# A two-layer attention and feed-forward kernel: its preparation divided anew among the engines, the context turned by VectorE

## The reference

```
x = x + L0_xattn(layernorm(x), ctx_512)     # 16 heads; this case's change is in its preparation and its last step
x = x + L0_ffn(layernorm(x))                # the top 64 of 256 rows of each sequence through a 256-1024-256 net
x = x + L1_xattn(layernorm(x), ctx_512)     # 16 heads of 16, causal
x = x + L1_ffn(layernorm(x))                # 8 experts and a shared one

def L0_xattn(hidden_q, kv_c):
    q_big = rope(einsum(hidden_q @ Wq.T, w_kc_q))        # 16 heads of 192
    kv_r  = kv_c * cos + rotate_half(kv_c) * sin         # the context, turned
    scores = (q_big @ W_qr) @ (kv_r @ W_kr).T
    ctx_lat = (softmax(scores) @ kv_r) @ w_kc_kv.T
    return ctx_lat @ Wo.T
```

## Time and profile before

| | |
|---|---|
| median of three runs | 1833.09 us (1830.51 to 1841.44) |
| profiled execution | 1842.96 us, span 1841.1 us |
| busy: TensorE (PE), VectorE (DVE) | 1665.8 us (90%), 1365.5 us (74%) |
| busy: ScalarE (ACT), GpSimd (POOL) | 993.2 us (54%), 941.7 us (51%) |
| mean granted TensorE clock | 0.944 of full speed |

### The profile page before, as it was taken

How to read it: one execution, slowest core, us unless ns; L and a number is a source line. 1 busy time by engine, 2 the same in 40 slices (tenths; PEclk the granted TensorE clock), 3 DMA queues, 4 the chain that set the end, 5 groups by cost and what they waited for, 6 DMA issues and landing times. The chain is left out here.

```text
span 1841.1 us, 48720 instructions
## 1 busy us (share of the span) xinstructions
PE 1665.8 (90%) x16216; PEld 1327.9 (72%) x16216; DVE 1365.5 (74%) x2952; ACT 993.2 (54%) x1983; POOL 941.7 (51%) x625
## 2 busy tenths in 40 slices
PE   6437999999999999999999999996958889997898
PEld 5334888888888888888888888886846445556676
DVE  6876888888888888888888888885664468884223
ACT  5233666666666666666666666662212356662111
POOL 2802777777777777777777777771000221211321
PEclk8557999999999999999999999998979889997999
DMA  9422122112112112122122124128410000004234
GB/s 269 149 63 65 51 61 79 51 56 82 49 59 84 49 57 79 53 60 78 50 65 71 53 67 139 51 73 258 138 53 2 22 26 12 11 12 167 90 122 155
DMA packets 150138, 144.14 MB, mean 78 GB/s; under 512 B 41290, under 2 KB 137208, under 8 KB 149584
## 3 DMA queue, kind: packets, MB, share of 16 engines
q1 hardware_dynamic: 144144, 135.33, 24.6%
q10 hardware_dynamic: 4416, 4.29, 0.7%
q0 software_dynamic: 1536, 3.99, 0.6%
HBM read 92.01 MB, written 33.98 MB: 68 GB/s over the span
## 5 line engine op out<-in xcount | busy, mean ns | idle before, releaser
L1059 POOL TENSOR_TENSOR c_rest<-c_prob 128x1024 f16<-128x1024 f32 (+1 forms) x513 | 796.1, 1572 | 315.4 <-ACT c_prob L902 302.7
L978 DVE TENSOR_REDUCE c_mxp<-c_psM 128x1 f32<-128x400 f32 (+1 forms) x1040 | 588.9, 573 | 114.4 <-PE c_psM L762 99.7
L902 ACT ACTIVATE c_prob<-c_psS,ln,c_exp_scale 128x1024 f32<-128x1024 f32 (+1 forms) x514 | 536.3, 1044 | 243.8 <-PE c_psS L778 238.8
L778 PE MATMUL c_psS<-c_q,c_kk 128*128 128x256 f16 (+1 forms) x3350 | 512.7, 272 | 1.7 <-ACT c_prob L902 1.6
L796 PE MATMUL c_psV<-c_vb,c_prob 128*128 128x129 f16 (+1 forms) x3328 | 396.5, 222 | 0.5 <-POOL c_rest L1059 0.5
L778 PEld LDWEIGHTS c_psS<-c_q,c_kk 128*128 128x128 f16 (+1 forms) x3350 | 321.7, 99 | 87.5 <-ACT c_prob L902 2.2
L799 PE MATMUL c_psV<-c_vb,c_rest 128*128 128x65 f16 (+1 forms) x3328 | 374.2, 193 | 0.0
L762 PE MATMUL c_psM<-c_kkm,c_q 128*128 128x400 f16 (+1 forms) x1040 | 347.5, 335 | 6.1 <-DVE c_mxp L978 3.9
L799 PEld LDWEIGHTS c_psV<-c_vb,c_rest 128*128 128x128 f16 (+1 forms) x3328 | 301.4, 99 | 22.1
L796 PEld LDWEIGHTS c_psV<-c_vb,c_prob 128*128 128x128 bf16 (+1 forms) x3328 | 305.3, 97 | 14.6 <-POOL c_rest L1059 0.7
L724 PE MATMUL c_psQ<-c_xb,c_w2s 128*128 128x256 f16 x1188 | 164.3, 275 | 4.2 <-DVE c_roped L946 2.5
(11 more groups left out here) (294 smaller groups left out, 2187.3 us busy)
## 6 DMA issues: line engine op xcount, KB each, us to landing
c_w2s<-w_scr SPq DMA_DIRECT2D x67, 256.0 KB, 2.6
acc_scr<-c_acc SPq DMA_DIRECT2D x128, 129.0 KB, 2.2
c_ms<-m_scr SPq DMA_DIRECT2D x67, 192.0 KB, 2.3
c_w2s<-w_scr SPq DMA_DIRECT2D x67, 128.0 KB, 2.0
kv<-acc_scr SPq DMA_DIRECT2D x4, 2064.0 KB, 10.3
d_acc<-acc_scr SPq DMA_DIRECT2D x4, 2064.0 KB, 8.3
m_w<-in_L_ffn_W SPq DMA_DIRECT2D x16, 352.0 KB, 4.2
c_vb<-V SPq DMA_DIRECT2D x27, 129.0 KB, 2.0
```

The source lines that it names most:

```text
L778: mm = pe.matmul(psS[g % 2][0:r, i * S:(i + 1) * S], src[:, (lo + i) * P:(lo + i) * P + r], mov[slot][:, :], start=(one == 0 and i % 2 == ...
L902: nc.scalar.activation(prob[g][0:r, 0:w], psS[g % 2][0:r, 0:w], ACT.Exp, bias=keep["ln1024"][0:r, :], scale=exp_scale[slot][0:r, :]).then_ ...
L978: nc.vector.tensor_reduce(mxp[:, st, c:c + 1], psM[:, st, 0:CHUNKS[c][1]], AX.X, ALU.max).then_inc(mx_done, 1)
L1059: nc.gpsimd.tensor_tensor(rest[g][0:r, 0:w], prob[g][0:r, 0:w], high[0:r, 0:w], ALU.subtract).then_inc(rest_done, 1)
```

## The change

In the preparation:
- the context's loads are moved up: batch 0 and the tables behind the first two groups of weights, batch 1 behind the third, the others ahead of Wo and w_kc_kv;
- VectorE takes the largest absolute values from the context as it arrives, before it is turned (`top_of`); GpSimd's maximum over partitions follows in the first block, and the key scale is made there too, with a factor of 1.4143 for what turning can add;
- ScalarE writes the high parts of the weights, and the copies and squares of m straight from PSUM; VectorE keeps the rests;
- GpSimd turns nothing any more; VectorE turns all 8 batches, behind the rests;
- the normalised x is made behind that, and the value products (`wvo`) are last on TensorE and VectorE, their store last on SP.

In the projection x is loaded by SP behind the second batch's sums, the wait for it stands in `add_rows`, and TensorE raises its starting semaphores before it waits for its loads.

The diff, cut to its core:

```diff
         def _(sp):
-            for g in range(H0 // 4):
+            def load_weights(g):
                 heads = slice(4 * g, 4 * g + 4)
                 sp.dma_start(wq[:, heads], t["L0_xattn_Wq"].rearrange("(h k) d -> k h d", h=H0)[:, heads]
                              ).then_inc(in_q[g], 16)
                 sp.dma_start(wkcq[:, heads], t["L0_xattn_w_kc_q"].rearrange("h k q -> k h q")[:, heads]
                              ).then_inc(in_q[g], 16)
...
-            sp.wait_ge(kv_zeroed, 1)
             def load_context(b):
...
+            load_weights(0)
+            load_weights(1)
+            sp.wait_ge(kv_zeroed, 1)
             load_context(0)
+            sp.dma_start(cosk[:], t["cosk"]).then_inc(in_t, 16)
+            sp.dma_start(sink[:], t["sink"]).then_inc(in_t, 16)
+            load_weights(2)
+            load_context(1)
+            load_weights(3)
+            sp.dma_start(ident[:], t["ident"]).then_inc(in_r, 16)
+            sp.dma_start(wqr[:], t["L0_xattn_W_qr"].rearrange("h (e q) r -> q h e r", e=2)).then_inc(in_r, 16)
+            sp.dma_start(wkr[:], t["L0_xattn_W_kr"].rearrange("h d r -> d h r")).then_inc(in_r, 16)
+            for b in range(2, B):
+                load_context(b)
             sp.dma_start(wo[:], t["L0_xattn_Wo"].rearrange("(c e) k -> e c k", e=P)).then_inc(in_o, 16)
             sp.dma_start(wkckv[:], t["L0_xattn_w_kc_kv"].rearrange("h k d -> k h d")).then_inc(in_o, 16)
-            for b in range(1, B):
-                load_context(b)
...
-            sp.wait_ge(w2p_done, 3 * H0)
+            sp.wait_ge(w_high, 3 * NP0)
+            sp.wait_ge(w_low, 3 * NP0)
             sp.dma_start(t["w2_scr"].rearrange("g p c -> p g c"),
                          wqk[:, 0:H0 * DK * DCQ].rearrange("p (g c) -> p g c", g=NP0)).then_inc(stored, 16)
-            sp.wait_ge(d_done, D_NM)
-            sp.dma_start(t["wvo_scr"], wvo[:]).then_inc(stored, 16)
...
+            sp.wait_ge(d_done, D_VO + N_VO)
+            sp.dma_start(t["wvo_scr"], wvo[:]).then_inc(stored, 16)
...
         @block.gpsimd
...
-            pool.wait_ge(in_t, 32)
-            h = DC // 2
-            for b in range(B):
-                r = rot[b % 2]
-                pool.wait_ge(in_k[b], 32)
-                if b >= 2:
-                    pool.wait_ge(roped, b - 1)
-                nc.gpsimd.tensor_tensor(r[:, :, 0:h], kv[:, b, :, h:DC], sink[:, :, 0:h],
-                                        ALU.mult).then_inc(rotated, 1)
-                nc.gpsimd.tensor_tensor(r[:, :, h:DC], kv[:, b, :, 0:h], sink[:, :, h:DC],
-                                        ALU.mult).then_inc(rotated, 1)
-                pool.wait_ge(rotated, 2 * b + 2)
-                nc.gpsimd.tensor_tensor(kv[:, b], kv[:, b], cosk[:], ALU.mult).then_inc(kv_turned, 1)
-                pool.wait_ge(kv_turned, b + 1)
-                if b < POOL_SUMS:
-                    nc.gpsimd.tensor_tensor(kv[:, b], kv[:, b], r[:], ALU.add).then_inc(roped, 1)
+            pool.wait_ge(amax_ready, B)
+            nc.gpsimd.partition_all_reduce(aall[:], amax[:], P, bass.bass_isa.ReduceOp.max
+                                           ).then_inc(aall_ready, 1)
...
         @block.tensor
         def _(pe):
...
-            pe.wait_ge(in_o, 32)
-            for g in range(H0 // 2):
-                n = A_WOT + g
-                pe.wait_ge(a_done, n - 3)
...
-                mm.then_inc(a_full, 1)
             for g in range(N_M):
...
-            for g in range(N_VO):
-                n = D_VO + g
-                pe.wait_ge(a_done, A_WOT + 2 * g + 2)
-                pe.wait_ge(d_done, n - 3)
+            pe.wait_ge(in_o, 32)
+            for g in range(H0 // 2):
+                n = A_WOT + g
+                pe.wait_ge(a_done, n - 3)
...
-                mm.then_inc(d_full, 1)
+                mm.then_inc(a_full, 1)
...
                 mm.then_inc(d_full, 1)
+            for g in range(N_VO):
+                n = D_VO + g
+                pe.wait_ge(a_done, A_WOT + 2 * g + 2)
+                pe.wait_ge(d_done, n - 3)
...
+                mm.then_inc(d_full, 1)
...
+            def split(h):
+                for out, rows in pieces(h, 0):
+                    nc.scalar.activation(out, rows, ACT.Copy, scale=w_scale[:, h:h + 1]).then_inc(w_high, 1)
+
             for g in range(H0 // 2):
                 n = A_RT + g
                 act.wait_ge(a_full, n + 1)
                 nc.scalar.activation(rT[:, 2 * g:2 * g + 2, :].rearrange("r h c -> r (h c)"),
                                      psA[n % 4][0:R0, :], ACT.Copy).then_inc(a_done, 1)
+                if g == 0:
+                    act.wait_ge(wscale_ready, 1)
+                split(2 * g)
+                split(2 * g + 1)
+            for g in range(N_M):
+                n = D_M + g
...
+                act.wait_ge(d_full, n + 1)
+                for u in range(2):
+                    h = 2 * g + u
+                    act.wait_ge(norms_ready, H0 + h)
+                    nc.scalar.activation(junk[0:HALF, 0:2 * DC], psD[n % 4][0:HALF, u * 2 * DC:(u + 1) * 2 * DC],
+                                         ACT.Square,
+                                         accum_out=norms[0:HALF, H0 + h:H0 + h + 1]).then_inc(norms_ready, 1)
+                nc.scalar.activation(m[:, 2 * g:2 * g + 2, :, :].rearrange("p h e d -> p (h e d)"),
+                                     psD[n % 4][0:HALF, 0:4 * DC], ACT.Copy).then_inc(d_done, 1)
...
-            act.wait_ge(d_done, D_M + N_M)
-            for h in range(H0):
-                act.wait_ge(norms_ready, H0 + h)
-                nc.scalar.activation(junk[0:HALF, 0:2 * DC], m[:, h, :, :].rearrange("p e d -> p (e d)"),
-                                     ACT.Square,
-                                     accum_out=norms[0:HALF, H0 + h:H0 + h + 1]).then_inc(norms_ready, 1)
             act.wait_ge(b2_ready, 1)
...
+            def top_of(b):
+                dve.wait_ge(in_k[b], 32)
+                nc.vector.tensor_reduce(amax[:, b:b + 1], kv[:, b], AX.XY, ALU.max,
+                                        apply_absolute_value=True).then_inc(amax_ready, 1)
+
+            top_of(0)
             dve.wait_ge(in_x, 16)
             layer_norm_stats(dve, nc, agg_done, x, stats, agg, NT)
             dve.sem_inc(var_ready, 1)
+            top_of(1)
+            top_of(2)
 
             dve.wait_ge(root_ready, 1)
             rstd_refined(nc, link, rstd[:], root[:], agg, tmp[:])
-            for j in range(NT):
-                nc.vector.tensor_scalar(x[:, j, :], x[:, j, :], agg[:, j, 0:1], rstd[:, j:j + 1],
-                                        ALU.subtract, ALU.mult).then_inc(xln_ready, 1)
+            for b in range(3, B - 2):
+                top_of(b)
 
...
-            dve.wait_ge(a_done, H0)
...
-            def split(h):
-                for out, rows in pieces(h, 0):
-                    nc.vector.tensor_scalar(out, rows, w_scale[:, h:h + 1], None, ALU.mult).then_inc(w2p_done, 1)
+            dve.sem_inc(wscale_ready, 1)
+            for b in range(B - 2, B):
+                top_of(b)
...
             def split_rest(h):
+                dve.wait_ge(w_high, 3 * (h // 2) + 1 + 2 * (h % 2))
                 for (out, rows), (high, _) in zip(pieces(h, 1), pieces(h, 0)):
                     nc.vector.scalar_tensor_tensor(out=out, in0=rows, scalar=w_scale[:, h:h + 1], in1=high,
-                                                   op0=ALU.mult, op1=ALU.subtract).then_inc(w2p_done, 1)
+                                                   op0=ALU.mult, op1=ALU.subtract).then_inc(w_low, 1)
 
             for h in range(H0):
-                split(h)
-            dve.wait_ge(w2p_done, 3 * NP0)
-            for g in range(N_M):
-                n = D_M + g
-                split_rest(2 * g)
-                split_rest(2 * g + 1)
-                dve.wait_ge(d_full, n + 1)
-                nc.vector.tensor_copy(m[:, 2 * g:2 * g + 2, :, :].rearrange("p h e d -> p (h e d)"),
-                                      psD[n % 4][0:HALF, 0:4 * DC]).then_inc(d_done, 1)
-            dve.wait_ge(m_cleared, 16)
-            for g in range(N_VO):
-                n = D_VO + g
-                dve.wait_ge(d_full, n + 1)
-                nc.vector.tensor_copy(wvo[:, 2 * g:2 * g + 2, :].rearrange("p g e -> p (g e)"),
-                                      psD[n % 4][:, :]).then_inc(d_done, 1)
-
+                split_rest(h)
+
+            half = DC // 2
+            dve.wait_ge(in_t, 32)
+            for b in range(B):
+                r = rot[b % 2]
+                nc.vector.tensor_tensor(r[:, :, 0:half], kv[:, b, :, half:DC], sink[:, :, 0:half], ALU.mult)
+                link(nc.vector.tensor_tensor(r[:, :, half:DC], kv[:, b, :, 0:half], sink[:, :, half:DC], ALU.mult))
+                link(nc.vector.tensor_tensor(kv[:, b], kv[:, b], cosk[:], ALU.mult))
+                link(nc.vector.tensor_tensor(kv[:, b], kv[:, b], r[:], ALU.add))
+
+            for j in range(NT):
```

(47 more changed lines are left out.)

56 lines of the change are left out of this document (23 added, 33 removed).

## The result

| | before | after |
|---|---|---|
| median of 20 executions each | 1841.83 us (1830.4 to 1849.1) | 1830.28 us (1823.61 to 1835.94) |
| profiled execution: time, span | 1842.96, 1841.1 us | 1830.17, 1828.3 us |

The ratio is 0.9941 (95% interval 0.9926 to 0.9956): the change saves 0.59%, some 10.9 us (the two medians are 11.6 apart), where 16.1 us were forecast. It is faster, but by less than 1%. The predicted 1817.0 us (range 1808 to 1826) misses the 1830.28 us, for two reasons that have to be kept apart. The base was wrong: the 1833.09 us of the record was a median of three runs, and twenty runs have 1841.83. And the gain was forecast too large.

A forecast was written before the change was run, and what follows sets the result against it. Layer 0's untouched attention fills most of the span; VectorE was taken to bound the preparation, VectorE and TensorE were read for the projection. 1833.1 - 9.3 (preparation) - 6.8 (projection) = 1817.0 us; own range 1812 to 1822, 8 in 10 1808 to 1826.

The forecast's parts named there:

- Weight scale ready, 44.2: Preparation: with two contexts and two tables loaded ahead of W_kr, the weights' scale is ready at 44.2, 13.8 us later.
- Weights at 1.36 us a pair on ScalarE, end of the rests 55.1: Preparation: ScalarE scales eight pairs of heads in 10.9 us; VectorE's subtractions end 0.5 us behind it.
- ScalarE sets the pace: Rival, preparation: ScalarE's pieces from SBUF don't overlap, weights take 14.8 us instead of 10.9, time 1820.9 us; chance 0.14.
- Turning, 3.27 us a context: Preparation: VectorE turns eight contexts, moved from GpSimd, in 26.2 us, ending at 81.3.
- From there to V: Preparation after turning: x, bound, xl, key scale, value products, store; V's first piece at 106.2 against 115.51, 9.3 us earlier.
- Projection, -6.8: Projection behind attention: earlier combinations and TensorE's batch 1 straight behind batch 0 save 6.8 us; bounds 2.4 and 7.5.
- TensorE stays low: Rival: low clock through the value products (+3.4 us) and again in the projection (1.7 us), time 1822 us; chance 0.12.
- The other side: Rival, preparation: VectorE's rests are slow by themselves, 36.8 us instead of 10.9, so +9.8 us, time 1843 us; chance 0.04.

The follow-up runs named there:

- the first experiments: After with before's projection: 1836.88 us, ratio 0.9962 against before (1846.13 us on that chip); before with after's projection: 1840.22 us, ratio 0.9964.

## Why the prediction missed, point by point

**The base failed first.** The prediction summed against the profiled execution (1842.96 us), noted that it was 0.5% long, and then subtracted the sum from 1833.09. Twenty executions of before show two bunches: four at 1830.4 to 1833.3 and sixteen at 1839.9 to 1849.1. Two of the three on record had come from the short bunch, and the profile from the long one. By the medians the miss of 13.3 us is 8.7 us of base (1841.83 where 1833.09 stood) and 4.6 us of gain (11.6 where 16.1 stood). Had the same sum been taken from 1841.83, the forecast would have been 1825.7: the measured 1830.28 would lie inside the range for 8 in 10, moved up by the same 8.7 us, and at the upper edge of the forecast's own. So the step that failed is the one before the sum: a median of three was taken as the base of a working whose every row came from an execution 9.9 us longer.

The gain, term by term, from the three pairs of profiles (16.1 forecast, 12.8 measured, 3.3 short): preparation 8.45 where 9.3 stood, projection 6.53 where 6.8 stood, and two stretches of the same code that the forecast put at nothing ("From there to attention nothing changes, so all of it is carried through"), the attention +0.87 and the tail +1.27, both within the scatter of one kernel.

What makes an execution of before short was not profiled and stays open. On the chip of the first experiments the five short ones (1832.6 to 1837.8 us) had a mean granted clock of 0.945 to 0.947 and the other twenty 0.939 to 0.946, so the clock goes along with it, but not strictly. It bears on the ratio: the mean of all twenty is 1840.8, and 1829.9 for after, 10.9 apart; without the four short ones of before it is 13.1, and the three pairs of profiles have 12.8.

**Weight scale ready, 44.2.** It was 42.9. W_kr's wait ended at 33.09 (34.5 forecast), so the two contexts and two tables ahead of it cost 4.4 us and not 5.8. The four contexts behind it came at the forecast pace: VectorE took up context 5 at 41.00, 7.9 us later, or 2.0 each. Right in kind, 1.3 us high.

**Weights at 1.36 us a pair on ScalarE, end of the rests 55.1.** The pace was 1.67, the end 56.8. The pieces from SBUF cost 1.2 us a pair where 0.88 stood in the sum (0.37, 0.26, 0.15 and three times 0.03); the upper bound of 1.85 held. The rival that ScalarE sets the pace is true as a fact, since VectorE waits 0.24 us in each of the last four pairs, but not at its price of 3.9 us: it cost 2.5 (eight times 0.31), and the earlier start gave 1.3 of it back; VectorE ended 0.8 us behind it, where 0.5 stood. By the Trainium skill's budget (ScalarE: Activation LUTs, Rules for kernel authors) a pair would have taken 2.26 us, an estimate; the rows decide, 1.67, between that and the forecast.

**Turning, 3.27 us a context.** It was 3.245: the two products of 416 elements 0.51 and 0.62 start to start, where 0.57 and 0.62 stood.

**From there to V.** Normalising 5.25 (5.3), bound and m until 92.0 (90.6), xl until 97.7 (96.1), key scale 1.33 (1.33), last wvo copy at 101.5 (100.1), V 4.6 us behind it (6.1), since the store landed after 3.9 us and not 5.0. The upper clock level came at 97.7 and not at 95.7; it held up nothing behind it, for VectorE's copies of wvo followed one another without a wait. Sum forecast 106.2, measured 106.07 in the first profile and 106.34 in the mean. That it fits so well is partly luck: the last copy was 1.4 us late, and the store and the barrier gave 1.5 back. The step that was off is on before's side: its V is at 114.79 in the mean of three, not 115.51. So -8.45 where -9.3 stood.

**Projection, -6.8.** First combination 2.4 us earlier in its block: 2.20 (4.60 to 2.40). Wait for x moved behind the sums: right, the second combination waits only for its own. The third load was to land at the same instant as before, 15.4 us behind its issue: it took 17.3 us from an earlier issue and ended at the forecast instant in the first profile; but in the second it took 18.7 and VectorE waited 4.44 us for it instead of 3.26. Over the profiles of all kernels with this projection it took either 17.3 to 17.5 or 18.7 to 18.8 us, and the projection is some 1.4 us longer in the second case. The projection's mean over three is -6.5 where -6.8 stood: right in mechanism and nearly in size.

**Rival "TensorE stays low".** Neither part came. The value products ran at the upper level from 97.7 on (96.5 and 97.4 in the other two profiles; they had begun at 96.3 to 96.9), and in the projection batch 0 had the low level as before, but batch 1's transposes took 1.91 us where before's took 2.95. A late loss in the tail had no place among the rivals; the runs show no mechanism for one, only scatter, and the scatter of 500 us of unchanged code should have stood in the range.

**The other side** fell as argued, and now by experiment: with GpSimd held back, the same rests took 11.3 us instead of 36.2, and with GpSimd's products put beside them they were slow again.

## What to carry to other kernels

When the median of few runs and the profiled execution of the same kernel are half a per cent apart, neither is the base: give the gain as a difference, and keep the gap between the two in the range. A gain of 16 us read off one pair of profiles was 14 in three pairs, so one pair carries some two microseconds of luck here. A pair of engines that read the same memory should be scheduled so that one works while the other waits for data; three contexts turned on GpSimd cost some 0.9 us beside VectorE's waits, while beside its work every single GpSimd product cost 1.7 us. And behind a change look for the new hole at the end of the block: 11.3 us more lay in two moved steps.
